# Sixteen 32x32 tiles for the random features and 128x32 tiles for the key-value state of a linear-attention block

## The chip, the cores and the metric

The kernel runs on one core of a Trainium2 chip. The metric is the device time of one execution in microseconds (us). Fewer are better.

## The reference

Input is x, two sequences of 2048 tokens of 256 features. Everything is 32-bit floating point. An adaptive layer norm, then a first half of three layers of causal linear attention, with a feed-forward part, then a second layer norm and a second half of two layers of windowed attention. Only the attention of the first half is touched by the change, and the per-feature scales of queries and keys of the second half. Cut to that:

```python
# first half, for each of 3 layers; 16 heads of 16 features, omega is 16 x 8
q, k, v = (out @ W + b, in heads, for W, b in (Wq,bq), (Wk,bk), (Wv,bv))
def favor(x, omega):                       # 16 features for each head and token
    xs = x * 16 ** -0.25
    u  = xs @ omega                        # 8 columns
    h  = 0.5 * sum(xs * xs)
    return concat([exp(u - h), exp(-u - h)]) * 16 ** -0.5
Qf, Kf = favor(q, omega), favor(k, omega)
S = running sum over tokens of Kf[m] * v[d];  z = running sum of Kf
a = (Qf . S) / (Qf . z + 1e-6)
out = layer_norm(out + a @ Wo + bo);  out = layer_norm(out + relu(out @ W1 + bf1) @ W2 + bf2)
# second half, for each of 2 layers
q = l2norm(q) * q_scale;  k = l2norm(k) * k_scale;  q, k = rotary_xpos(q, k)
```

## The kernel before

The program is written instruction by instruction, with an own order for each engine and semaphores between them. The tokens of the first half go in 24 blocks (n = 0 to 23: 8 blocks of 512 tokens for each of three layers), those of the second half in 64 units of 128 tokens. Nothing is planned at run time: the order on an engine is the order of the calls in its part of `build` (TensorE from line 613, ScalarE, VectorE, GpSimd and the DMA queue of SyncE after it), and for blocks 6 to 21 it is one loop body.

Of one block, TensorE does this, and works besides on the feed-forward part of the block before the last (`up` and `down`, laid between the attention's calls as filling):

- `proj(n, i)`, i = 0 to 3: six matmuls each into PSUM bank i. Banks 0 and 1 hold the keys' two halves of 128 features (m = 0, 1), banks 2 and 3 the queries'. A product in float32r is made of three matmuls on a high and a low part (`mm3`).
- ScalarE's `operands(n, i)` (lines 1901 to 1904) adds the bias and makes for each bank two tiles `OPS[i]`, A and B: of the 128 features 64 are kept as they are beside their 64 squares. Partitions change places in it, so it takes four activations of 64 partitions. It signals `a_sq`.
- `values(n, i)`: the values into banks 0 and 1; VectorE's `add_bv` (line 3185) writes them to `VP` and signals `d_v`.
- `favor(n, i, bank)`: u - h and -u - h for 128 of the features. Two matmuls of true fp32 with 128 rows and 64 columns on 512 tokens each. Their weights are `OM`: 128 x 128 numbers of omega, its negative, and -1/8 where a square enters. GpSimd's `features_of` makes `OM` once a layer. Order on the banks: 2, 3 for the keys, 0, 1 for the queries. It signals `e_fv`.
- ScalarE's `features(n, i, bank)` (lines 1913 to 1919): one exponential for each bank of keys (`FK`), three for each of queries (`FQ`). It signals `a_fe`.
- `attn_out` of the block before, `turn_k` (transposes of `FK`, line 477, copied to `KS` by ScalarE, line 1948), then for j = 0 to 3 `scores(n, j)` (32 rows x 128 columns, four row groups), which VectorE masks into `U` (line 3175), and `sums(n, j)`.
- `sums(n, j)` works in bank 4: two matmuls with the state `SBD`, then two that add the tile's keys times values to the state (weights `KS`, 128 x 128, moving `VP`, 128 columns; into columns 256 to 511; only the 16x16 blocks on the diagonal are wanted), then sixteen matmuls of 128 rows x 32 columns with `VP` and `U`. VectorE's `state` (line 3167) multiplies columns 256 to 511 with a block mask into `TMP`, and GpSimd (line 4627) adds that to `SBD`. For every sixteenth tile there is no update.

A float32 matmul stands in the trace as two records of MATMUL and two of LDWEIGHTS, a float32r one and a transpose as one of each.

```python
            mm(e, PS[0:64, bank, :], OM[:, l % 2, 0:64], OPS[i][0], True)
            mm(e, PS[64:128, bank, :], OM[:, l % 2, 64:128], OPS[i][1], True).then_inc(*e_fv.up(n, i))
```

Between the halves SyncE's queue (lines 5387 to 5400) loads the second half's first weights (`load_piece`, line 5286), tables of the rotation (`load_table`, line 5372) and the scales (`load_scales`, line 5385, 12 DMAs into `QSB`). GpSimd's `table(u)` (line 4814) multiplies a table with `QSB`; it waits for all 12. It stands in GpSimd's order before roundings of the last feed-forward part (`RL`, line 4615).

Of the kernel before, what the change touches and what calls it, by code (L numbers as in the profile page):

```python
# [41 lines left out]
def build(nc, ctx, ins, out):  # L42
# [47 lines left out]
    QSB = sb("QSB", [128, 2, 256])  # L90
# [21 lines left out]
    GG = sb("GG", [128, 6, 512])  # L112
# [11 lines left out]
    RSLOT = (0, 1, 2, 0, 2, 1)  # L124

# [38 lines left out]
    p_om = ev("p_om", by(range(3), R2))  # L164
# [54 lines left out]
    s_bb = ev("s_bb", by(range(3), range(11)), 16)  # L219
# [147 lines left out]
    def hidden(q, hb):  # L367
        return (KT, PR, PT)[hb // 2][:, hb % 2, :] if q == NQ - 1 else GG[:, hb, :]
# [6 lines left out]
    def residual_of(q):  # L375
        return T2 if q == NQ - 1 else GG[:, 4:6, :]
# [37 lines left out]
    def _(e):  # L414
# [13 lines left out]
        def proj(n, i):  # L428
            m, nm = i % 2, "wk" if i < 2 else "wq"
            if n > 0:  # L430
                e.wait_ge(*d_am.at(n - 1, 1))
            need_weights(e, piece_of(n // 8, nm))
            for k in range(2):
                e.wait_ge(*a_x.at(n, k))
                e.wait_ge(*d_x.at(n, k))
                t = mm3(e, PS[:, i, :], [a[:, 256 * k + 128 * m:256 * k + 128 * m + 128] for a in wt(nm, 0, 512)], xt(0, k, 0, 512), k == 0)
# [69 lines left out]
        def sums(n, j):  # L506
# [105 lines left out]
        values(0, 0)  # L612
        modulate(4)
        modulate(5)
        values(0, 1)
        favor(0, 0, 2)
        favor(0, 1, 3)
        favor(0, 2, 0)
        favor(0, 3, 1)
# [19 lines left out]
        favor(1, 0, 2)  # L639
        favor(1, 1, 3)  # L640
        favor(1, 2, 0)
        favor(1, 3, 1)
# [27 lines left out]
        favor(2, 0, 2)  # L670
        favor(2, 1, 3)
        favor(2, 2, 0)
        favor(2, 3, 1)
# [34 lines left out]
        values(3, 0)  # L708
        up(1, 2)
        values(3, 1)  # L710
        favor(3, 0, 2)
        favor(3, 1, 3)
        favor(3, 2, 0)
        favor(3, 3, 1)
# [40 lines left out]
        favor(4, 0, 2)  # L755
        favor(4, 1, 3)
        favor(4, 2, 0)
        favor(4, 3, 1)
# [38 lines left out]
        favor(5, 0, 2)  # L797
        favor(5, 1, 3)
        favor(5, 2, 0)
        favor(5, 3, 1)  # L800
# [27 lines left out]
        for n in range(6, 22):  # L828
# [7 lines left out]
            down(m, 0)  # L836
            up(m, 2)
            down(m, 1)
            values(n, 1)
            favor(n, 0, 2)  # L840
            favor(n, 1, 3)
            favor(n, 2, 0)
            favor(n, 3, 1)
# [273 lines left out]
        favor(22, 0, 2)  # L1117
        favor(22, 1, 3)
        favor(22, 2, 0)
        favor(22, 3, 1)  # L1120
# [38 lines left out]
        favor(23, 0, 2)  # L1159
        favor(23, 1, 3)  # L1160
        favor(23, 2, 0)
        favor(23, 3, 1)
# [723 lines left out]
    def _(e):  # L1886
# [4 lines left out]
        def operands(n, i):  # L1891
            l, m = n // 8, i % 2
            lo, hi = slice(0, 64), slice(64, 128)
            col = BC[:, l % 2, (2 if i < 2 else 0) + m:(2 if i < 2 else 0) + m + 1]
            if i == 0:
                e.wait_ge(*s_bb.at(l, 10))
# [3655 lines left out]
```

## Time and profile before

| | us |
|---|---|
| median of 3 executions | 2650.11 |
| lowest, highest | 2649.51, 2653.05 |
| the profiled execution, its own time | 2656.85 |
| its span in the profile | 2655.1 |
| TensorE busy in it | 2580.7 (97%) |

The profile is of one execution. Its page and its views give busy times of each engine, in all or in a stretch; groups of instructions with their mean duration; the chain of work that ended last; and the instructions in order of time, in which neighbours of a kind are merged (a row "x12" begins with its first and its length goes to the end of the last). A matmul's record is longer than the distance to the next, since matmuls are pipelined: starts are compared, not ends.

### The profile page before, as it was taken

Reading aid. Unit: us, or ns where it says so; the run is one execution under the profiler, and the core shown is the slowest. Engines: PE = TensorE matmul, PEld = TensorE weight load, DVE = VectorE, ACT = ScalarE, POOL = GpSimd, SP = SyncE. Lnnn points to the kernel's source line nnn. Section 1 sums busy time; section 2 is a strip of 40 time slices with the busy share of each in tenths; the row PEclk is TensorE's granted clock in tenths of the full one; section 3 lists DMA queues with packets and bytes.
Section 4 is the critical chain, followed back from the end, with each engine's and each line's share of the span. In section 5 each row is a group of like instructions: output and inputs, shape, how many; then the busy total and the mean of one; then the engine's idle time right before and its main releaser. Section 6 shows DMA issues by size and latency. Waiting matters only on the chain.

```text
span 2655.1 us, 61404 instructions
## 1 busy us (share of the span) xinstructions
PE 2580.7 (97%) x21288; PEld 2131.3 (80%) x21288; DVE 2119.8 (80%) x5244; ACT 1545.6 (58%) x3137; POOL 1426.2 (54%) x1406
## 2 busy tenths in 40 slices
PE   7899999999999999999898999999999999999998
PEld 4688888888888888888786788888888887888886
DVE  5688877787677777888899888888898887888775
ACT  3454445444554455444446777777767777777772
POOL 2253443444343345444476766666666666776664
PEclk9899999999999999999999999999999999999999
DMA  3100000010000010000111000000110110110001
GB/s 93 33 17 10 17 2 17 9 35 6 1 1 8 12 31 25 18 17 26 47 50 52 29 12 19 16 14 19 31 35 23 34 35 22 35 32 26 27 29 48
DMA packets 78976, 67.17 MB, mean 25 GB/s; under 512 B 15800, under 2 KB 73272, under 8 KB 78680
## 3 DMA queue, kind: packets, MB, share of 16 engines
q1 hardware_dynamic: 78680, 63.25, 8.1%
q8 instruction: 182, 2.98, 0.5%
q14 instruction: 114, 0.93, 0.1%
HBM read 49.18 MB, written 12.58 MB: 23 GB/s over the span
## 4 chain that ended last, share of the span: by engine, by line
PE 91%; DVE 3%; issue 2%; ACT 1%; POOL 1%; SPq 0%; DMA 0%; DVEq 0%; ACTq 0%; POOLq 0%
PE PS L274 81%; PE PS L982 4%; PE PS L944 1%; PE PS L935 1%; PE PS L1012 1%; PE PS L487 1%; PE PS L425 1%; PE PS L477 1%; PE PS L893 1%; DVE PS L3583 1%; PE PS L1042 0%; ACT PR L2244 0%; DVE U L3175 0%; DVE SM L3556 0%; DVE SQ L3563 0%
## 5 line engine op out<-in xcount | busy, mean ns | idle before, releaser
L2244 ACT ACTIVATE PR<-PS,SM 128x256 f32<-128x256 f32 (+1 forms) x512 | 280.3, 559 | 137.2 <-DVE SM L3588 136.8
L1930 ACT ACTIVATE FB<-PS,BC 128x512 f32<-128x512 f32 x192 | 133.4, 695 | 326.5 <-PE PS L274 188.0
L3175 DVE TENSOR_TENSOR U<-PS,CST 128x512 f32<-128x512 f32 x384 | 238.2, 683 | 42.1 <-PE PS L274 41.7
L4615 POOL TENSOR_TENSOR RL<-FB,RH 128x512 fp32r<-128x512 f32 x96 | 126.1, 1313 | 236.0 <-DVE RH L3153 236.0
L274 PE MATMUL PS<-W2H,RH 128*128 128x256 f32 x768 | 226.0, 294 | 6.9 <-POOL RL L4615 6.9
L4837 POOL TENSOR_TENSOR SM<-SM,COL 128x8 f32<-128x8 f32 x128 | 225.6, 1763 | 10.7
L3583 DVE CUSTOM_DVE_ANT_0 PS<-PS,MSK 128x256 f32<-128x256 f32 (+1 forms) x512 | 202.6, 436 | 30.0 <-PE PS L274 28.9
L274 PE MATMUL PS<-W2H,RL 128*128 128x256 f32 x768 | 215.8, 281 | 0.0
L274 PE MATMUL PS<-W2L,RH 128*128 128x256 f32 x768 | 215.6, 281 | 0.0
L4627 POOL TENSOR_TENSOR SBD<-SBD,TMP 128x256 f32<-128x256 f32 x84 | 64.5, 768 | 217.2 <-DVE TMP L3167 217.2
L274 PEld LDWEIGHTS PS<-W2H,RH 128*128 128x128 f32 x768 | 145.1, 189 | 29.6 <-issue 25.0
L274 PE MATMUL PS<-VAH,XBH 128*128 128x512 f32 x384 | 163.3, 425 | 1.0 <-ACT SQ L2193 0.6
L274 PE MATMUL PS<-X1H,W1H 128*128 128x512 f32 x384 | 160.6, 418 | 3.1 <-ACT FB L1930 2.4
L1938 ACT COPY NUM<-PS 128x256 f32<-128x256 f32 x96 | 36.1, 376 | 200.9 <-DVE TMP L3167 173.4
L274 PE MATMUL PS<-X1L,W1H 128*128 128x512 f32 x384 | 151.7, 395 | 0.0
L274 PE MATMUL PS<-VAL,XBH 128*128 128x512 f32 x384 | 151.4, 394 | 0.0
L274 PE MATMUL PS<-VAH,XBL 128*128 128x512 f32 x384 | 151.4, 394 | 0.0
L274 PE MATMUL PS<-X1H,W1L 128*128 128x512 f32 x384 | 151.2, 394 | 0.0
L274 PE MATMUL PS<-KT,QT 64*128 64x256 f32 (+1 forms) x1024 | 142.4, 396 | 8.9 <-ACT PT L2257 6.2
L4619 POOL TENSOR_TENSOR X0L<-NUM,X0H 128x512 fp32r<-128x512 f32 x48 | 65.5, 1384 | 156.4 <-ACT X0H L1944 156.4
L274 PEld LDWEIGHTS PS<-W2L,RH 128*128 128x128 f32 x768 | 145.3, 189 | 2.4
L982 PE MATMUL PS<-CST,PR 128*128 128x128 f32 x992 | 137.6, 274 | 7.7 <-ACT PR L2244 7.6
(265 smaller groups left out, 8711.2 us busy)
## 6 DMA issues: line engine op xcount, KB each, us to landing
PX<-in_L_attn_x SPq DMA_DIRECT2D x16, 512.0 KB, 4.0
TB<-in_k_rot SPq DMA_DIRECT2D x64, 128.0 KB, 2.3
SG<-in_L_attn_W SPq DMA_DIRECT2D x24, 256.0 KB, 2.7
xp_scratch<-PX SPq DMA_DIRECT2D x8, 512.0 KB, 2.9
xs_scratch<-X SPq DMA_DIRECT2D x64, 64.0 KB, 1.5
ZS<-xs_scratch SPq DMA_DIRECT2D x16, 256.0 KB, 2.8
GG<-xp_scratch SPq DMA_DIRECT2D x7, 512.0 KB, 3.7
out<-GG SPq DMA_DIRECT2D x7, 512.0 KB, 2.9
```

Of the source, the lines that this page charges most:

```text
L274: return e.matmul(o, l, r, start=start, stop=True, skip_group_check=True)
L425: t = e.transpose(PS[:, 2 + k, 128 * j:128 * j + 128], X[:, 4 * c + j, 128 * k:128 * k + 128], IDN)
L982: m = e.transpose(PS[:, 3 + par, a:a + 128], PR[:, par, a:a + 128], IDN)
L1930: e.activation(FB[:, hb % 2, :], PS[:, 5, :], ACT.Relu, bias=BC[:, l % 2, 4 + hb:5 + hb]).then_inc(*a_re.up(n, hb))
L1938: e.copy(NUM[:, :, 128 * j:128 * j + 128], PS[:, 4, 0:256].rearrange("p (m q) -> p m q", m=2)).then_inc(*a_nu.up(n, j))
L2244: t = e.activation(PR[:, par, 256 * i + lo:256 * i + hi], PS[:, 3 + par, 256 * i + lo:256 * i + hi], ACT.Exp, bias=S[:, 40 + 2 * g + i:41 ...
L3175: e.tensor_tensor(heads(U[:, u % 6, :], 4), heads(PS[:, g, :], 4), bcast(CM, 4), ALU.mult).then_inc(*d_mk.up(n, u))
L3583: t = e.tensor_tensor_reduce(o, o, MSK[:, z:z + hi - lo], 1.0, NEG, ALU.add, ALU.max, S[:, 32 + 2 * g + i:33 + 2 * g + i])
L4615: e.tensor_tensor(RL[:, r, :], FB[:, 0, :], RH[:, r, :].bitcast(F), ALU.subtract).then_inc(*p_rl.up(n, hb))
L4619: e.tensor_tensor(X0L[:, k, :], NUM[:, k, :], X0H[:, k, :].bitcast(F), ALU.subtract).then_inc(*p_al.up(n, k))
L4627: e.tensor_tensor(SBD[:, (tile + 1) % 2, :, :], SBD[:, tile % 2, :, :], TMP[:, :, :], ALU.add).then_inc(*p_sd.up(n, j))
L4837: e.tensor_tensor(o, a, MHALF.broadcast_to([128, 8]), ALU.pow).then_inc(*h_rs[i].up(u))
```

## The change

- The columns of Wq and Wk are stored in another order (`split_parts`), so that `proj(n, i)` makes 32 features of each half of the queries and of the keys. It is the same number of matmuls; the rounding of these two weights takes two instructions for one.
- `operands` takes two activations of 128 partitions for four of 64. The biases' columns are loaded in that order (13 small DMAs for a layer where there were 11).
- `favor(n)` is one call: for each of the four row groups (r = 2, 3, 0, 1) and each bank's operands (c = 0 to 3) one 32x32 matmul with omega's block on the plain features, and then sixteen more with the -1/8 block on the squares, into the same banks. It begins when all operands and both halves of the values are there. `OM` shrinks to a block that repeats, so `features_of` takes one instruction for two.
- In `sums` the update of the state is eight matmuls of 128 rows x 32 columns on 32 columns, into 64 columns of bank 4 for 256. `state` reads these 64 columns four times each.
- `values(n, 1)` goes before the calls that stood between it and `values(n, 0)` (in block 0 the last two products of the modulation, in blocks 3 and 6 to 21 one or two feed-forward calls).
- `QSB` moves behind `GG` (which gives its first plane to `G0`, at the place of `QSB`). Layer 0's scales are loaded before block 16, layer 1's at unit 4 of the second half, after `load_norm(0)`. `table(u)` waits for the six DMAs of layer 0 only while u < 32.

```diff
     def split_parts(p):
+        if phase == 1 and at < 1024:
+            def places(w, k):
+                return w[:, 512 * k:512 * k + 512].rearrange("p (s t m f) -> p t m s f", s=4, t=2, m=2)[:, at // 512, :, :, :]
+            return [(places(WQH, k), places(WQL, k), s[:, 256 * k:256 * k + 256].rearrange("p (m s f) -> p m s f", m=2, s=4)) for k in range(2)]
...
-        def favor(n, i, bank):
+        def favor(n):
             l = n // 8
-            e.wait_ge(*p_om.at(l, 1))
-            e.wait_ge(*a_sq.at(n, i))
-            if i < 2:
-                e.wait_ge(*a_sq.at(n, 2 + i))
-            else:
-                e.wait_ge(*d_v.at(n, i - 2))
-            mm(e, PS[0:64, bank, :], OM[:, l % 2, 0:64], OPS[i][0], True)
-            mm(e, PS[64:128, bank, :], OM[:, l % 2, 64:128], OPS[i][1], True).then_inc(*e_fv.up(n, i))
+            e.wait_ge(*p_om.at(l))
+            for i in range(4):
+                e.wait_ge(*a_sq.at(n, i))
+            for i in range(2):
+                e.wait_ge(*d_v.at(n, i))
+            for r in BANKS:
+                for c in range(4):
+                    mm(e, PS[32 * c:32 * c + 32, r, :], OM[32 * r:32 * r + 32, l % 2, 0:32], OPS[c][0][32 * r:32 * r + 32, :], True)
+            for i, r in enumerate(BANKS):
+                for c in range(4):
+                    t = mm(e, PS[32 * c:32 * c + 32, r, :], HO[32 * r:32 * r + 32, 0:32], OPS[c][1][32 * r:32 * r + 32, :], False)
+                t.then_inc(*e_fv.up(n, i))
...
                 for m in range(2):
-                    mm(e, PS[:, 4, 256 + 128 * m:384 + 128 * m], KS[:, j // 2, D * (j % 2) + 128 * m:D * (j % 2) + 128 * m + 128],
-                           value_places(VP[:, j, :])[:, 4 * m:4 * m + 4, :, :], not started and m == 0)
+                    for g in range(4):
+                        a = D * (j % 2) + 128 * m + 32 * g
+                        mm(e, PS[32 * g:32 * g + 32, 4, 256 + 32 * m:288 + 32 * m], KS[:, j // 2, a:a + 32],
+                               value_places(VP[:, j, :])[:, 4 * m + g, :, :], not started and m == 0)
...
             A, B = OPS[i]
-            e.activation(A[lo, :], PS[lo, i, :], ACT.Identity, bias=col[lo, :])
-            e.activation(B[hi, :], PS[hi, i, :], ACT.Identity, bias=col[hi, :])
-            e.activation(A[hi, :], PS[lo, i, :], ACT.Square, bias=col[lo, :])
-            e.activation(B[lo, :], PS[hi, i, :], ACT.Square, bias=col[hi, :]).then_inc(*a_sq.up(n, i))
+            e.activation(A, PS[:, i, :], ACT.Identity, bias=col)
+            e.activation(B, PS[:, i, :], ACT.Square, bias=col).then_inc(*a_sq.up(n, i))
...
-                e.wait_ge(*t_qs.at(11))
-                e.tensor_tensor(TB[:, u % 2, :], TB[:, u % 2, :], QSB[:, u // 32, :], ALU.mult).then_inc(*h_tb.up(u))
+                e.wait_ge(*t_qs.at(11 if u >= 32 else 5))
+                e.tensor_tensor(TB[:, u % 2, :], TB[:, u % 2, :], QSB[:, 1 - u // 32, :], ALU.mult).then_inc(*h_tb.up(u))
...
+        load_scales(0)
         for n in range(16, 21):
...
         load_piece(P2 + 1)
         load_table(0)
-        load_scales(0)
-        load_scales(1)
         load_piece(P2 + 2)
...
                 load_norm(0)
+                load_scales(1)
```

## Rows read from the trace of the kernel before

**Rows 1.** The page: the span, and busy times of the engines

```profile
span 2655.1 us, 61404 instructions
...
PE 2580.7 (97%) x21288; PEld 2131.3 (80%) x21288; DVE 2119.8 (80%) x5244; ACT 1545.6 (58%) x3137; POOL 1426.2 (54%) x1406
```

**Rows 2.** Busy times of PE, PEld, DVE, ACT, POOL in most of the first half

```profile
110.00:1250.00 1140.00, 1137.92 (x10753) 944.96 (x10749) 891.90 (x1905) 561.26 (x929) 485.06 (x454) 1.00 0.05 15
```

**Rows 3.** The chain that ended last, 110 to 1250 us, by line

```profile
by line: PE PS L274 94.5%; PE PS L487 1.9%; PE PS L425 1.7%; PE PS L477 1.6%; ACT FB L1930 0.1%; DVE U L3175 0.1%; issue 0.1%
```

**Rows 4.** TensorE in order of time, block 11: start, length, tiles, rows*columns

```profile
621.11 2.80 PE L274 MATMUL PS<-U,OM 128*64 128x512 f32 x12
623.73 1.03 PE L274 MATMUL PS<-KS,OM 128*64 128x512 f32 x4
624.69 0.50 PE L274 MATMUL PS<-X1H,W1H 128*128 128x512 f32 x1
...
629.87 0.48 PE L274 MATMUL PS<-X1H,W1H 128*128 128x512 f32 x1
...
631.42 1.15 PE L274 MATMUL PS<-FQ,FK 32*128 32x256 f32 x16
```

**Rows 5.** Line 274 (source view), the first 0.2 us of scores(11, 0)

```profile
L274 PE MATMUL PS<-FQ,FK x4: 478/478/478, 631.4 to 631.4; 32*128 32x256 f32 x4
```

**Rows 6.** TensorE in order of time in sums(11, 1)

```profile
642.40 0.61 PE L274 MATMUL PS<-VP,KS 128*128 128x128 f32 x4
642.95 1.08 PE L274 MATMUL PS<-U,VP 128*32 128x128 f32 x32
```

**Rows 7.** ScalarE in order of time, block 11

```profile
610.14 0.69 ACT L1901 ACTIVATE U<-PS,BC 64x512 f32<-64x512 f32 x1 [0.77 <-PE PS L274]
...
620.62 0.68 ACT L1904 ACTIVATE KS<-PS,BC 64x512 f32<-64x512 f32 x1
...
623.08 1.26 ACT L1919 ACTIVATE FK<-PS,COL 128x512 f32<-128x512 f32 x2
...
627.07 0.74 ACT L1915 ACTIVATE FQ<-PS,COL 128x512 f32<-128x512 f32 x1
627.64 0.74 ACT L1930 ACTIVATE FB<-PS,BC 128x512 f32<-128x512 f32 x1
```

**Rows 8.** VectorE in order of time between two masks

```profile
639.48 2.48 DVE L3175 TENSOR_TENSOR U<-PS,CST 128x512 f32<-128x512 f32 x4
...
644.09 0.42 DVE L3167 TENSOR_TENSOR TMP<-PS,CST 128x256 f32<-128x256 f32 x1 [1.08 <-PE PS L274]
...
645.17 2.48 DVE L3175 TENSOR_TENSOR U<-PS,CST 128x512 f32<-128x512 f32 x4 [0.32 <-PE PS L274]
```

**Rows 9.** TensorE in order of time, block 1

```profile
76.30 1.08 PE L274 MATMUL PS<-U,OM 128*64 128x512 f32 x4 [0.72 <-ACT U L1904]
...
87.57 0.60 PE L477 MATMUL PS<-CST,FK 128*128 128x128 f32 x4
89.04 1.15 PE L274 MATMUL PS<-FQ,FK 32*128 32x256 f32 x16 [0.88 <-ACT KS L1948]
```

**Rows 10.** SyncE's queue in order of time between the halves

```profile
1307.90 0.48 SPq L5372 DMA_DIRECT2D TB<-in_k_rot  x1
1308.42 1.50 SPq L5385 DMA_DIRECT2D QSB<-in_L_ffn_q_scale  x3
...
1312.81 1.38 SPq L5385 DMA_DIRECT2D QSB<-in_L_ffn_k_scale  x3
```

**Rows 11.** GpSimd in order of time between the halves

```profile
1318.96 0.88 POOL L4814 TENSOR_TENSOR TB<-TB,QSB 128x256 f32<-128x256 f32 x1 [15.70 <-DMA QSB<-in_L_ffn_k_scale]
1319.80 1.44 POOL L4615 TENSOR_TENSOR RL<-FB,RH 128x512 fp32r<-128x512 f32 x1
```

**Rows 12.** TensorE between the halves, the end of its longest gap

```profile
1321.49 0.55 PE L274 MATMUL PS<-W2H,RH 128*128 128x256 f32 x1 [6.85 <-POOL RL L4615]
```

**Rows 13.** DMAs of 1303 to 1325 us: size, median us to landing

```profile
TB<-in_k_rot SPq DMA_DIRECT2D x1, 128.0 KB, 5.4
```

More of the change, by code:

```diff
@@ L89, in build @@
     TB = sb("TB", [128, 2, 256])
-    QSB = sb("QSB", [128, 2, 256])
+    G0 = sb("G0", [128, 512])
     MSK = sb("MSK", [128, 384])
@@ L111, in build @@
     HTH, HTL = sb("HTH", [128, 2, 512], FR), sb("HTL", [128, 2, 512], FR)
-    GG = sb("GG", [128, 6, 512])
+    GG = sb("GG", [128, 5, 512])
+    QSB = sb("QSB", [128, 2, 256])
     PS = ctx.enter_context(nc.psum_tensor("PS", [128, 8, 512], F))
@@ L162, in build @@
     d_rh, d_rl = ev("d_rh", by(S24, R8)), ev("d_rl", by(S24, (1, 3, 5, 7)))
-    p_om = ev("p_om", by(range(3), R2))
+    p_om = ev("p_om", by(range(3)))
     p_xb, p_hb, p_al, p_zq = (ev(f"p_{k}", by(S24, R2)) for k in ("xb", "hb", "al", "zq"))
@@ L218, in build @@
     s_row = [ev(f"s_row{i}", by(range(3)), 16) for i in range(7)]
-    s_bb = ev("s_bb", by(range(3), range(11)), 16)
+    s_bb = ev("s_bb", by(range(3), range(13)), 16)
     s_x = ev("s_x", [("p", c) for c in S8] + [("r", n) for n in CH3], 16)
@@ L375, in residual_of @@
     def residual_of(q):
[L376 removed]
+        return T2 if q == NQ - 1 else GG[:, 3:5, :]
     def gate_bank(q, hb):
@@ L612, in _ @@
         values(0, 0)
+        values(0, 1)
         modulate(4)
         modulate(5)
[L615 to L619, printed above, removed]
+        favor(0)
         turn_k(0, 0)
@@ L638, in _ @@
         values(1, 1)
[L639 to L642, printed above, removed]
+        favor(1)
         attn_out(0, 0)
@@ L669, in _ @@
         up(0, 2)
[L670 to L673, printed above, removed]
+        favor(2)
         up(0, 3)
@@ L708, in _ @@
         values(3, 0)
+        values(3, 1)
         up(1, 2)
[L710 to L714, printed above, removed]
+        favor(3)
         up(1, 3)
@@ L754, in _ @@
         up(2, 3)
[L755 to L758, printed above, removed]
+        favor(4)
         attn_out(3, 0)
@@ L796, in _ @@
         up(3, 3)
[L797 to L800, printed above, removed]
+        favor(5)
         attn_out(4, 0)
@@ L836, in _ @@
             down(m, 0)
+            values(n, 1)
             up(m, 2)
             down(m, 1)
[L839 to L843, printed above, removed]
+            favor(n)
             up(m, 3)
@@ L1116, in _ @@
         down(20, 1)
[L1117 to L1120, printed above, removed]
+        favor(22)
         up(20, 3)
@@ L1158, in _ @@
         down(21, 1)
[L1159 to L1162, printed above, removed]
+        favor(23)
         up(21, 3)
@@ L5360, in store_scaled, with load_scales @@
             e.dma_start(xp_d[4 * c:4 * c + 4].rearrange("t p d -> p t d"), PX.rearrange("p i (t d) -> p (i t) d", t=2)).then_inc(*s_xp.up(n))
+        def load_scales(l):
+            for i, nm in enumerate(("q", "k")):
+                v = ins[f"L0_ffn_{nm}_scale"][l:l + 1, :]
+                for z, (a, b, n) in enumerate(((0, 0, 64), (64, 32, 32), (96, 0, 32))):
+                    e.dma_start(QSB[:, 1 - l, 128 * i + a:128 * i + a + n], v[:, b:b + n].broadcast_to([128, n])).then_inc(*t_qs.up(6 * l + 3 * i + z))
+        load_scales(0)
         for n in range(16, 21):
@@ L5379, in load_norm @@
                 e.dma_start(B2[:, i, :], ins["L0_ffn_" + nm][l:l + 1, :].broadcast_to([128, D])).then_inc(*t_b2.up(l, i))
-        def load_scales(l):
-            for i, nm in enumerate(("q", "k")):
-                v = ins[f"L0_ffn_{nm}_scale"][l:l + 1, :]
-                for z, (a, b, n) in enumerate(((0, 0, 64), (64, 32, 32), (96, 0, 32))):
-                    e.dma_start(QSB[:, l, 128 * i + a:128 * i + a + n], v[:, b:b + n].broadcast_to([128, n])).then_inc(*t_qs.up(6 * l + 3 * i + z))
         load_again(21)
@@ L5507, in constants @@
     sign = np.where(i % 16 < 8, 0.5, -0.5).astype(f)
-    other = (((i[:, None] + 64) % 128) // 16 == i[None, :] // 16).astype(f) * f(-0.125)
-    cst = np.stack([np.eye(128, dtype=f), blk, other, (i[:, None] <= i[None, :]).astype(f), blk * sign[None, :]], axis=1)
+    pairs = (i[:, None] % 32 // 16 == i[None, :] % 32 // 16).astype(f)
+    cst = np.stack([np.eye(128, dtype=f), blk, pairs * f(-0.125), (i[:, None] <= i[None, :]).astype(f), pairs * sign[None, :]], axis=1)
     c = np.arange(32)
```

40 lines of the change are left out of this document (21 added, 19 removed).

## The prediction

> **What bounds the kernel now.** I read the page first: TensorE is busy for 97% of the span, no other engine for more than 80% [rows 1]. Its busy time is that of pipelined records, so the chain of waits was read next. From 110 to 1250 us it is TensorE's alone: its lines make up 99.7% of the chain [rows 3], and it is busy for 1137.9 of 1140 us, with VectorE at 78%, ScalarE at 49% and GpSimd at 43% [rows 2]. So in blocks 2 to 23 time taken out of TensorE's stream is time won, until another engine's chain becomes the later one. The other stretches have limits of their own: block 1 waits for ScalarE [rows 9], and between the halves TensorE stands for 6.85 us for a rounding by GpSimd [rows 12], which stood behind a DMA of the scales [rows 11]. The second half proper is not touched.
>
> **The features on TensorE.** Before, eight fp32 matmuls leave 16 records, from 621.11 us to 624.69, where the next call starts: 3.58 us [rows 4]. A slot is the distance between starts on one tile. The first twelve records take 2.80 us and the next four start at 623.73, so twelve records in six slots took 2.62 us: 0.43 us a slot, two column tiles at once. Eight slots are 3.44 us; the rest is a first weight load and the change of tile shape at the end. After, 32 matmuls leave 64 records. If all sixteen tiles run beside one another, that is two matmuls a tile, two records each: 4 slots, 1.72 us. That tiles do run beside one another is seen for four: in `scores` 16 records of 32 rows take 1.15 us together [rows 4], and four begin within the same 0.1 us, each 0.48 us long [rows 5]. No row has both row and column tiles. Bounds: 1.72 us (all sixteen at once), and above no concurrency beyond a few tiles (rivals below). I take 4 slots, since with four row tiles and with four column tiles [rows 4, 6] nothing but the slots is seen. I add 0.1 us for starting sixteen tiles in turn and 0.1 us for weight load and change of shape (an estimate: the 3.58 us above held 0.14 for that): 1.94 us, 1.64 us less for each block.
>
> A rule of the Trainium skill speaks against this. The page "TensorE: Matmul & The Clock Gate", Part 3 on packing small matmuls, says that matmuls start and end strictly in program order. By that rule the two passes of a matmul, on one tile, would hold up all that is behind them; what it would cost is a rival. By it the 16 records of `scores` could not overlap by four, and rows 4 and 5 show that they do.
>
> **What the block loses again.** ScalarE's exponentials follow each other by 0.57 us (from the first `FK` at 623.08 to the last `FQ` at 627.07 are seven steps [rows 7]). Before they began 1.97 us after `favor`. After, all four banks come at once, about 2.1 us after it. So they are hardly earlier, while TensorE is 1.64 us earlier. The relu behind them ended at 628.38 [rows 7] and TensorE wanted it at 629.87 [rows 4]: slack 1.49 us. It becomes 1.49 - 1.64 - 0.15 = -0.3 us. I count 0.3 us of new wait a block. Net 1.34 us. The operands themselves go from 16 to 8 activations of 0.70 us a block, done before from 610.14 to 621.30 [rows 7], just in time for `favor`. The freed 5.6 us are off the path (ScalarE is at 49%) and pay only in block 1. They also mean that waiting for all operands at once costs nothing: they are then bounded by `proj`, which ends over 5 us before. The values' second half moves ahead of feed-forward calls, so `d_v` is not late either; what moves behind it is filling whose inputs were there.
>
> **The state's update.** Before, 4 records from 642.40 to the next start at 642.95: 0.55 us, of it 0.44 for four slots of 0.11 and 0.1 for the change of shape, which stays but moves in front [rows 6]. After, 16 records on four column tiles, 4 slots. A slot of 128 columns is about 0.11 us; here are 32 columns. Bounds: a quarter of that, 0.03 us a slot, or no less than now, 0.11 us (no gain); nothing is added, since the number of slots stays. I take 0.04 us, nearer the quarter, as in `favor` and `sums` the slot goes with the columns (0.43 us for 512, 0.11 for 128): 0.28 us less for each tile. VectorE has 0.32 and 1.08 us idle in a round of `sums` [rows 8] and its masks ended at 641.96, 0.99 us before they were wanted at 642.95 [rows 6, 8]; four tiles take 1.1 us from a block but each has a round of its own to catch up. So I keep it whole. `state` reads 64 columns four times for 256 once: 0.42 us as before [rows 8].
>
> **The two first blocks.** Block 0: ScalarE sets the pace; keys' exponentials start about 1 us later, the last ends about 0.2 us later. Block 1: TensorE was ready at 75.6 us (76.30 less 0.72 of waiting) and reached `scores` at 89.04 [rows 9]. After, operands are ready; the last exponential ends 2.15 + 7 x 0.57 + 0.74 = 6.9 us after the start, and the last transposes, their copy and the start of `scores` take 89.04 - 87.57 = 1.47 us as before [rows 9]: 84.0 us, 5 us won.
>
> **Between the halves.** The 12 DMAs of the scales hold SyncE's queue from 1308.42 to 1314.19 [rows 10], and GpSimd waited until 1318.96 for the last of them [rows 11]. After, GpSimd waits only for the table, issued at 1307.90 [rows 10]; it lands 5.4 us later, 1313.3 [rows 13]. So its product and the rounding behind it come 5.7 us earlier. The gap is 6.85 us [rows 12]. Bounds 0 to 5.7 us: VectorE is nearly full just there and may not follow. I take 4.5 us. The six DMAs put at unit 4 take 2.9 us of the queue (half of 5.8), at a place where the queue waits for the end of the first half; nothing there is wanted soon. The six put before block 16 stand before reloads of x, wanted long after.
>
> **At the start** two more DMAs (0.48 us each by the same rows) and four more rounding instructions: 0 to 1.5 us, I take 0.5.
>
> **Sum.** Features, blocks 2 to 23: 22 x 1.34 = 29.5. State, 82 of their 88 tiles: 82 x 0.28 = 23.0. Block 1: 5.0, block 0: -0.2. Handover 4.5, start -0.5. Together 61.3 us. The profiled execution of 2656.85 us would take 2595.5; the median of the runs lies 6.74 us below it, so 2650.1 - 61.3 = 2588.8 us. That is 2.3%; a measurement here tells some 0.2% (5 us) from no change.
>
> **Rivals.**
> - *Another chain takes over* (10%). ScalarE's or VectorE's chain behind `favor` costs 1.3 us a block, not 0.3: 22 us more, 2611. For it: the slack of 1.49 us is used up. Against: all engines but TensorE are under 80%.
> - *Features not faster* (9%). Only eight tiles at once: 8 slots, as before, with no new waits. 61.3 - 29.5 - 1.6 = 30 us won, 2620.
> - *Row groups one after the other* (3%), the case on the other side. Four column tiles run together but the next row group waits for both passes: 8 groups x 2 slots x 0.43 = 6.9 us, 3.3 us more a block. 2620 + 24 x 3.3 = 2699. It decides from 1.25 us a block on (30 / 24), a `favor` of 4.8 us. For it: no row mixes the two tilings.
> - *Strict order* (2%). A tile's second record waits for its first, and only the next tile's first runs beside it: 33 slots, 14.2 us, 10.6 us more a block, 2874 us. Against: rows 4 and 5. It is the rule named above.
> - *The change does not shorten what it seems to*: the state's slots stay at 0.11 us. That is 23 us, and lies in the range.
>
> **Numbers.** The forecast has 76%: 2588.8, and alone a range of 2577 to 2605 (state at 0.03 us a slot, no new waits, the whole gain at the handover: 11 us lower; no gain at the handover and half of the state's: 16 us higher). To leave out 2 in 10 at most I reach to the first rival: 2574 to 2612. Faster by over 0.2%: 0.94 (forecast, first two rivals); slower by over 0.2%: 0.05; within: 0.01.
>
> **What would show it.** 64 records of 32*32 a block, from first to next call 1.9 us; rows of `KS` as 128*32 in about 0.2 us; 96 activations of 128x512 in place of 64x512 for each of two lines; the relu behind the exponentials within 0.3 us of its use; no wait of GpSimd for `QSB`. A `favor` over 3 us, TensorE busy under 98% in the first half, or a gap of over 3 us left between the halves would show steps wrong.

## The result, and the profile of the changed kernel

The changed kernel takes 2636.76 us (median of 4 runs, 2633.62 to 2638.52), the kernel before 2650.36 beside it: a ratio of 0.9946, 95% interval 0.993 to 0.9962. It is faster by 13.6 us where 61.3 had been forecast, and 48 us above the forecast of 2588.8. The profiled execution took 2638.52 us, its span 2636.7. The page after, with the line that answers to [rows 1]:

```profile
span 2636.7 us, 65564 instructions
...
PE 2530.9 (96%) x23520; PEld 2096.4 (80%) x23520; DVE 2130.5 (81%) x5253; ACT 1403.9 (53%) x2945; POOL 1425.5 (54%) x1406
```

TensorE's busy time fell by 49.8 us and the span by only 18.4: the rest came back as idle time. The stretch of [rows 2] shows where:

```profile
110.00:1250.00 1140.00, 1111.26 (x12796) 928.92 (x12796) 911.47 (x1933) 442.72 (x768) 495.45 (x459) 0.99 0.05 15
```

Of 1140 us TensorE is idle for 28.7, where it was idle for 2.1 before, and the granted clock is 0.99 of full, not 1.00. What TensorE waited for from 150 to 1250 us, all of it before and the three largest waits after (engine, line, releaser: us in total, times, longest us):

```profile
PE PS L274 <- ACT FB L1930: 0.2, 1, 0.2
```

```profile
PE PS L276 <- DVE VP L3169: 22.8, 17, 3.3
PE PS L276 <- issue: 1.7, 2, 0.8
PE PS L276 <- DVE X1L L3011: 1.6, 2, 1.2
```

One new wait makes up nearly all of it: 17 times TensorE stands for line 3169, `add_bv`, VectorE's bias add that takes the values out of PSUM. It stands in front of the features, which now write into those banks all at once. In this text a *gap* is the distance between the start of the features and the start of the last matmul before them; it is 0.21 us where TensorE doesn't wait. Before, every block from 6 to 23 had 0.21. After, the ordinary blocks have 0.79, and blocks 6, 10, 11, 18, 20, 21 and 23 have 2.15 to 3.57; only block 22 kept 0.21. TensorE in block 12 after:

```profile
665.82 0.28 PE L276 MATMUL PS<-W2H,RL 128*128 128x256 f32 x1
666.61 0.63 PE L276 MATMUL PS<-U,OM 32*32 32x512 f32 x3 [0.52 <-DVE VP L3169]
...
666.72 0.61 PE L276 MATMUL PS<-KS,OM 32*32 32x512 f32 x1
667.04 0.62 PE L276 MATMUL PS<-U,OM 32*32 32x512 f32 x3
...
667.47 0.84 PE L276 MATMUL PS<-U,CST 32*32 32x512 f32 x3
...
667.91 0.61 PE L276 MATMUL PS<-KS,CST 32*32 32x512 f32 x1
...
668.36 0.59 PE L276 MATMUL PS<-KS,CST 32*32 32x512 f32 x1
668.88 0.50 PE L276 MATMUL PS<-X1H,W1H 128*128 128x512 f32 x1
```

The features themselves do what the change says. Sixteen tiles start within 0.11 us (666.61 to 666.72), the next record on the first tile 0.43 us later, and from first to next call it is 2.27 us where it was 3.58 [rows 4].

The state's update, which answers to [rows 6] (block 12):

```profile
685.56 0.61 PE L276 MATMUL PS<-FQ,SBD 128*128 128x128 f32 x4
686.10 0.33 PE L276 MATMUL PS<-VP,KS 128*32 128x32 f32 x16
686.25 1.18 PE L276 MATMUL PS<-U,VP 128*32 128x128 f32 x32
```

From the start of the `KS` records to the next start it is 0.15 us where it was 0.55. From the start of the `SBD` records in front of them to `KS` it is 0.54 us, where it was 0.44 before. That makes about 0.29 us less a tile.

Between the halves, answering to [rows 11] and [rows 12]: GpSimd waits for the table itself, and TensorE's gap shrank from 6.85 us to 1.89.

```profile
1300.27 0.74 POOL L4796 TENSOR_TENSOR TB<-TB,QSB 128x256 f32<-128x256 f32 x1 [10.59 <-DMA TB<-in_k_rot]
1300.97 1.71 POOL L4597 TENSOR_TENSOR RL<-FB,RH 128x512 fp32r<-128x512 f32 x1
```

```profile
1302.94 0.35 PE L276 MATMUL PS<-W2H,RH 128*128 128x256 f32 x1 [1.89 <-POOL RL L4597]
```

**Why VectorE is late.** VectorE in order of time, in block 11 before and in block 12 after (for both, the second `VP` line is the values' second half):

```profile
616.41 1.66 DVE L3014 SCALAR_TENSOR_TENSOR Z<-Z,ST,BB 128x256 f32<-128x256 f32 x4
618.16 1.67 DVE L3022 SCALAR_TENSOR_TENSOR X<-Z,ST,BB 128x256 f32<-128x256 f32 x4
621.22 0.76 DVE L3185 TENSOR_TENSOR VP<-PS,BB 128x256 f32<-128x256 f32 x2 [1.38 <-PE PS L274]
```

```profile
660.66 0.76 DVE L3169 TENSOR_TENSOR VP<-PS,BB 128x256 f32<-128x256 f32 x2 [4.27 <-PE PS L276]
661.33 1.67 DVE L2997 SCALAR_TENSOR_TENSOR Z<-Z,ST,BB 128x256 f32<-128x256 f32 x4
663.09 2.71 DVE L3005 SCALAR_TENSOR_TENSOR X<-Z,ST,BB 128x256 f32<-128x256 f32 x4
665.72 0.74 DVE L3169 TENSOR_TENSOR VP<-PS,BB 128x256 f32<-128x256 f32 x2
```

Before, the second half was written from 621.22 to 621.98, that is 0.87 us *after* the features had begun at 621.11 [rows 4], and nobody minded: only the fourth pair waited for it, 2.6 us in. After, the first matmul waits for it. What VectorE itself waited for before was TensorE: its products were done at 619.83, and then it stood idle for 1.38 us until the values' matmuls had come. The change moves these matmuls forward, so the add could follow the products at once and end at about 620.6, 0.5 us ahead of the features (an estimate from these rows: 619.83 + 0.76). So in an ordinary block the eight products of `norm2_b` ahead of the add leave it in time, with little to spare. In blocks 6, 10, 18 and 21 they don't: there VectorE was not idle before the add in the kernel before either. In block 10, where weight splits come on top, the products ended 0.2 us after the features' start (566.84):

```profile
565.36 1.67 DVE L3022 SCALAR_TENSOR_TENSOR X<-Z,ST,BB 128x256 f32<-128x256 f32 x4
566.95 0.76 DVE L3185 TENSOR_TENSOR VP<-PS,BB 128x256 f32<-128x256 f32 x2
```

The second thing is that after, in block 12, the four products of `X` take 2.71 us instead of 1.67. The source view of line 3005 for those four, and of the same line before:

```profile
L3005 DVE SCALAR_TENSOR_TENSOR X<-Z,ST,BB x4: 478/482/1519, 663.1 to 664.3; 128x256 f32<-128x256 f32 x4
```

```profile
L3022 DVE SCALAR_TENSOR_TENSOR X<-Z,ST,BB x4: 479/480/484, 618.2 to 619.4; 128x256 f32<-128x256 f32 x4
```

One product of the four took 1519 ns, the others 480. GpSimd ran `X0L` at the time (a view of each kernel, GpSimd in order of time):

```profile
664.09 2.84 POOL L4601 TENSOR_TENSOR X0L<-NUM,X0H 128x512 fp32r<-128x512 f32 x2 [6.82 <-ACT X0H L1927]
```

```profile
622.02 2.75 POOL L4619 TENSOR_TENSOR X0L<-NUM,X0H 128x512 fp32r<-128x512 f32 x2 [9.39 <-ACT X0H L1944]
```

Before, ScalarE had 16 activations for the operands and came to the cast that feeds `X0L` only at 621.33, so GpSimd began 0.9 us after the features. With 8 activations ScalarE casts at 663.39, and GpSimd begins 2.5 us ahead of them, beside VectorE's products. The Trainium skill says of this, on the page "SBUF — State Buffer", section "SBUF: two separate sides", that VectorE and GpSimd share a pair of ports, and that a VectorE operation with two inputs in SBUF and a GpSimd operation that reads SBUF exclude each other for a whole instruction. The trace agrees in kind: one product, with inputs `Z` and `BB`, is longer by 1.04 us, against 1.4 us of one `X0L` that had begun 0.19 us before it (GpSimd's spans are rough). These 1.04 us are more than the 0.5 us to spare in an ordinary block; in blocks 11 and 20 two products take about 1.5 us each beside `X0L`, and the gap is 2.16 and 2.15.

**The clock.** Behind the long gaps TensorE's granted clock falls to half (1.2 GHz). Three of seven such places after block 5 (stretch, length, busy times, and PEclk as the number before the last two):

```profile
556.00:563.00 7.00, 6.07 (x69) 2.77 (x70) 2.55 (x6) 2.16 (x4) 0.00 (x0) 0.52 0.35 42
614.00:618.00 4.00, 4.00 (x53) 2.00 (x37) 1.08 (x1) 1.80 (x4) 0.00 (x0) 0.58 0.02 4
1092.00:1096.00 4.00, 4.00 (x39) 1.95 (x9) 1.94 (x2) 2.66 (x5) 0.00 (x0) 0.59 0.05 17
```

The features there take 3.13 to 4.00 us instead of 2.27. Before, the granted clock from 110 to 1250 us was 1.00 of full [rows 2].

### The profile page after: what moved, and what is told of

It is laid out like the page before. It is cut to its first block, busy times and chain, and to the rows that moved or that the text cites. A ratio compares the mean times of both kernels' runs of the same rounds, so it can differ in the third digit from the quotient of the medians.

```text
span 2636.7 us, 65564 instructions
## 1 busy us (share of the span) xinstructions
PE 2530.9 (96%) x23520; PEld 2096.4 (80%) x23520; DVE 2130.5 (81%) x5253; ACT 1403.9 (53%) x2945; POOL 1425.5 (54%) x1406
## 4 chain that ended last, share of the span: by engine, by line
PE 49%; DVE 5%; issue 3%; POOL 2%; ACT 1%; DMA 0%; SPq 0%; DVEq 0%; ACTq 0%; POOLq 0%
PE PS L276 41%; PE PS L974 4%; PE PS L936 1%; PE PS L927 1%; PE PS L1004 1%; PE PS L885 1%; DVE PX L3005 1%; DVE PS L3567 1%; PE PS L1034 1%; ACT PR L2227 0%; DVE ST L2986 0%; DVE SQ L3547 0%; DVE SM L3540 0%; POOL ST L4566 0%; DVE Z L2997 0%
## 5 line engine op out<-in xcount | busy, mean ns | idle before, releaser
L4597 POOL TENSOR_TENSOR RL<-FB,RH 128x512 fp32r<-128x512 f32 x96 | 126.2, 1315 | 221.5 <-DVE RH L3136 221.5
L276 PEld LDWEIGHTS PS<-W2H,RL 128*128 128x128 f32 x768 | 144.9, 189 | 0.0
L4832 POOL TENSOR_TENSOR OTL<-OO,OTH 128x512 fp32r<-128x512 f32 x64 | 82.9, 1295 | 105.4 <-ACT OTH L2263 105.4
```

The lines of the kernel that those rows point to most:

```text
L276: return e.matmul(o, l, r, start=start, stop=True, skip_group_check=True)
L4597: e.tensor_tensor(RL[:, r, :], FB[:, 0, :], RH[:, r, :].bitcast(F), ALU.subtract).then_inc(*p_rl.up(n, hb))
L4832: e.tensor_tensor(OTL[:, :], OO[:, :], OTH[:, :].bitcast(F), ALU.subtract).then_inc(*h_ol.up(u))
```

## The experiments

Theory A: the late bias add of the values, an order on VectorE, costs the missing gain. A2: it is late because GpSimd's earlier `X0L` slows VectorE. B: VectorE's queue is simply full, so that what is moved back is wanted as much. C: the sixteen tiles themselves bring the lower clock. D: moving the values' matmuls is to blame.

### vp_first: the values' bias add first

In VectorE's loop over blocks 6 to 21:

```
+            add_bv(n, 1)
             splits(n, "v")
             if z >= 0: norm2_b(z)
-            add_bv(n, 1)
```

> Blocks 6 to 21: VectorE writes the second half of VP before the weight splits and the second norm's two products, nothing else. Theory A (TensorE waits before favor because that write is late in VectorE's queue, and its clock falls to half after the longest of these waits): the waits before favor, 22 us over 0.21 us a block in these 16 blocks, go, and with them five or six of the seven stretches at half clock, 7 us in favor and some more behind it: 28 to 35 us less, about 2605. Theory B (VectorE's queue is simply full, so what moves back is wanted as much): under 8 us less. Theory C (the clock falls because of the 32x32 tiles, whatever the wait): the waits go, 22 us less, but the stretches at half clock stay.

Measured: 2605.89 us (4 runs), ratio 0.983 (0.9814 to 0.9846). TensorE's waits for `VP` from 150 to 1250 us:

```profile
PE PS L276 <- DVE VP L3169: 4.7, 2, 3.0
```

The two left are blocks 3 and 23, outside the loop. In blocks 6 to 22 every gap is 0.21, the features take 2.28 us, and the clock never falls. 31 us came back by moving one line of VectorE's order; the gaps of blocks 6 to 21 sum to 3.3 us instead of 25.6, and their features take 7.2 us less. A is confirmed. B, with under 8 us, and C fall: the same tiles run at full clock. VectorE in block 12:

```profile
651.89 0.76 DVE L3169 TENSOR_TENSOR VP<-PS,BB 128x256 f32<-128x256 f32 x2 [0.34 <-PE PS L276]
652.56 3.72 DVE L3005 SCALAR_TENSOR_TENSOR X<-Z,ST,BB 128x256 f32<-128x256 f32 x4
```

The products are even slower here (3.72 us), and nobody waits for them: the slow products hurt only through what stood behind them.

### x0l_late: GpSimd waits for the products

```
+            e.wait_ge(*d_nb.at("2", z))
             low_attention(w, 0)
```

> Blocks 6 to 21: GpSimd's low part of the attention (X0L) waits until VectorE has done the second norm; nothing else. Theory A2 (GpSimd's X0L beside it stretches VectorE's four products X from 1.67 to 2.7 or 3.7 us, and that is what makes VP late): these products take 1.7 us again, the wait before favor goes from 0.58 to about 0 in the ordinary blocks and falls by 1 to 2 us in the others, 10 to 20 us less. Rival (the products are long for another reason, or VP is late because of what stands in front alone): under 5 us, products as long as before.

Measured: 2611.51, ratio 0.9853 (0.9838 to 0.9867).

```profile
650.22 1.67 DVE L3005 SCALAR_TENSOR_TENSOR X<-Z,ST,BB 128x256 f32<-128x256 f32 x4
651.81 0.74 DVE L3169 TENSOR_TENSOR VP<-PS,BB 128x256 f32<-128x256 f32 x2
```

With GpSimd held back the products take 1.67 us again. The add comes in time in ordinary blocks and in blocks 11 and 20 (gap 0.21); in block 12 it ends at 652.55, 0.6 us ahead of the features at 653.16. Blocks 6, 10, 18 and 21 have 0.86, 1.45, 1.32 and 1.43, without a fall of the clock: there the add is late without `X0L` too (in block 6 two products are slow beside another GpSimd operation, as before the change). So in most blocks both are needed for the loss, an order that leaves about half a microsecond, and a neighbour that takes 1 us. Either edit alone mends most. The gain of 25 us is larger than the 10 to 20 expected: 18.0 of it are gaps of blocks 6 to 21, and 7.3 their features, which the clock had made longer.

### vp_first_x0l_late: both

> Both edits. Theory A with A2: little more than the better of the two, under 5 us, since either takes the wait before favor away in ordinary blocks. If VectorE's time is what binds (theory B), the two add up, since only this one gives VectorE time back.

Measured: 2607.32, ratio 0.9836 (0.9821 to 0.985), no clear difference from the first: nothing is left for the second edit to win.

### values_late: the values' matmuls where they were before

In TensorE's loop `values(n, 1)` stands behind `down(m, 1)` again, right ahead of the features.

> Blocks 6 to 21: the values' second half is again made right before favor, as in the kernel before. X0L then starts later, so VectorE's products are short again, but favor now waits for both halves of VP, which come about 1.1 us after the values. Theory A: a wait of 0.9 to 1.3 us in each block and none of 2 to 3.5, so no stretch at half clock in these blocks: between 8 us less and 3 us more than the change. Theory that the earlier values cost nothing: 15 us more.

Measured: 2621.05, ratio 0.9892 (0.9877 to 0.9907): 15.7 us better than the change, and my expectation of about no difference was wrong. All blocks 6 to 21 now have a gap of 1.22 to 1.45 us, more than the 0.79 of ordinary blocks in the change, but no long ones, and no half clock behind them. VectorE's `X` products take 1.67 us there in block 12 and the others like it. So the sum of the gaps of these blocks is 20.1 us instead of 25.6, and the features of the same blocks take 7.4 us less: 12.9 of the 15.7 us. D holds in part: with VectorE's order as it was, the move cost 15.7 us. It isn't to blame by itself, since vp_first keeps it and is 15.2 us faster than this run: the matmuls have to be forward *with* their add.

### before_reordered: the same order in the kernel before

> The kernel before with the same move in VectorE's order as helped the change: the bias add of the values' second half ahead of the weight splits and norm products in blocks 6 to 21. If that order is only a debt that the change made due (the features used to wait for the second half of the values at their fourth pair alone), nothing is won here: the gap before the features is 0.21 us already, 2649 to 2651.5. If the order is better by itself, 2640 or less, and the change's own features part is then overrated by that.

Measured: 2653.11 (10 runs) against 2650.05, ratio 1.0012 (1.0003 to 1.0021). The order is worth nothing, or slightly less than nothing, by itself (2649 to 2651.5 was expected). It was a debt that the change made due.

### state_alone, handover_alone, vp_first_no_state: the terms priced

`state_alone` is the kernel before with the change's two hunks for the state's update (TensorE's eight matmuls and VectorE's mask on compact blocks).

> The kernel before, with only the state's update of the change: eight matmuls of 32 output columns on 128x32 tiles in place of two of 128, and the mask read from the compact blocks. The prediction's term is 82 updates x 0.28 us = 23.0 us, all of it on TensorE's own path, so 2627.5 us. In the change's trace the group of KS matmuls went from 0.54 to 0.15 us and the one after it from 0.44 to 0.54, 0.29 net: by that 2626.8. If the shorter update makes another engine late (VectorE's masks or the scans), less than 18 us comes out and the gap stands before the state's or the score's matmuls. No lower clock is expected, since nothing before the features changes.

Measured: 2623.83, ratio 0.9901 (0.9885 to 0.9917): 26.3 us. Block 11's matmuls:

```profile
630.35 0.33 PE L274 MATMUL PS<-VP,KS 128*32 128x32 f32 x16
630.49 1.06 PE L274 MATMUL PS<-U,VP 128*32 128x128 f32 x32
```

From the features of block 2 to those of block 23 it takes 1113.0 us where the kernel before takes 1137.2, 24.2 less. In that stretch 79 tiles have an update (84 less the last tile of blocks 3, 7, 11, 15 and 19), so it is 0.31 us for each, a little more than the 0.29 of the rows. Another 11 updates stand in blocks 0, 1 and 23.

`handover_alone` is the kernel before with the scales' new place and times.

> The kernel before, with only the scales moved: QSB at its new place, six loads before the sixteenth block and six after the first norm load, G0 apart from GG. The prediction's term is 4.5 us, from TensorE's gap of 6.85 us before the second half's first rotated operands. In the change's trace that gap was 1.89 us. Expected 2645.7 to 2646.2. A rival: the six loads on SyncE ahead of block sixteen's delay a load there, then the gain is under 3 us and a block about 16 is longer.

Measured: 2645.55 (12 runs), ratio 0.9981 (0.9973 to 0.999): 4.6 us, where the term was 4.5. The interval is wide beside it, about 2.6 to 7.2 us.

`vp_first_no_state` is the reordered kernel with the state's update of before.

> The change with VectorE's bias add of the values' second half ahead of the norm products and weight splits in blocks 6 to 21, and with the state's update as before the change: so it holds the features' part and the handover's. With the state's term at 23 to 24 us it should take 2605.9 + 23.5 = 2629.4 us. Below the kernel before by 21: 4.5 of handover, the rest features, where the prediction had 29.5 + 5.0 of block 1; what is missing are the gaps before the features in blocks 1, 3 and 23 (5.6, 2.1 and 3.3 us) and the features' 2.27 us in place of 1.94. If the two parts help each other or stand in each other's way it differs from 2629.4 by more than 3.

Measured: 2629.06, ratio 0.9923 (0.9905 to 0.9941), and 2629.4 was expected: the parts add up. Less the handover the features' part is worth 16.5 us, with the gaps of blocks 1, 3 and 23 still in it.

### vp_all: blocks 1, 3 and 23 as well

```
-        norm2_b(0)
-        splits(3, "v")
         add_bv(3, 0)
         add_bv(3, 1)
+        norm2_b(0)
+        splits(3, "v")
```
the same in block 23, and in block 1 `add_bv(1, 1)` ahead of `modulate_b(2)`.

> As the reordered kernel of blocks 6 to 21 (2605.9 us), and the same in blocks 1, 3 and 23: the bias add of the values stands ahead of the next block's modulation in block 1, and ahead of the norm products and weight splits in blocks 3 and 23. Gaps before the features there were 5.61, 2.07 and 3.30 us; if each falls to about 0.3 and block 23's features run at full clock (2.28 against 3.76), 5 + 1.8 + 3.0 + 1.5 = 11 us come back: 2595. If another wait stands right behind the add (the casts of ScalarE, the scans), only a part does: 2600 to 2604. If the delayed norm products hold up turning of x in the next block, a block period after 3 or 23 grows.

Measured: 2598.17 (2596.95 to 2598.75), ratio 0.9802 (0.9788 to 0.9815), the fastest kernel of the study: 52.0 us below the one before, 38.6 below the change. Its page:

```profile
span 2595.2 us, 65564 instructions
...
PE 2516.7 (97%) x23520; PEld 2089.7 (81%) x23520; DVE 2134.4 (82%) x5253; ACT 1403.5 (54%) x2945; POOL 1428.2 (55%) x1406
```

No wait for `VP` is listed from 150 to 1250 us. Gaps: 2.52 in block 1, 0.48 in block 3, 0.21 in 23, whose features take 2.28. It is 3 short of the hope. In block 1 TensorE now waits 2.2 us for ScalarE's operands. So it does in the change's own profile, where that gap is 2.52 too; in vp_first and five other profiles with the same block 1 it waits for the values and the gap is 5.6. No run tells what decides between the two, so no gain is shown for the edit in block 1.

### split_wait and split_vp_all: the features in two halves

Row groups 2 and 3 (both passes) wait for the operands alone; the waits for `d_v` stand in front of row groups 0 and 1.

```
-            for i in range(2):
-                e.wait_ge(*d_v.at(n, i))
-            for r in BANKS:
+            for h in range(2):
+                if h:
+                    for i in range(2):
+                        e.wait_ge(*d_v.at(n, i))
+                for r in BANKS[2 * h:2 * h + 2]:
...
```

> The change with VectorE's order untouched, but the features in two halves: row groups 2 and 3 (both passes, 16 matmuls) wait for the operands alone, and the waits for the two halves of the values stand in front of row groups 0 and 1. One half takes 4 slots of 0.43 = 1.7 us. In ordinary blocks (values late by 0.58 us) the second half enters while the first runs, on other rows: features of about 2.3 us with no gap, so 0.6 us a block back; in blocks 6, 10, 11, 18, 20, 21 and 23, late by 2 to 3.4 us, 1.7 us of it is hidden, and the late half adds its own 1.7, so about 0.6 back too, but TensorE is no longer idle for over 1.9 us and the clock should hold, which gives 1 to 1.7 us more in each. Sum: 16 x 0.6 + 7 x 1.9 = 23: 2614. If a wait for all operands at once is not what cost the time, it stays at 2637. If the halves don't overlap, ordinary blocks lose about 1.1 us and it is over 2645.

Measured: 2630.44, ratio 0.9918 (0.9903 to 0.9934): 6.3 us below the change, not 23.

> The fastest so far (2598.2 us, the values' bias add first in blocks 1, 3, 6 to 21 and 23) with the features in halves as well. Nothing is late there but in blocks 1 (2.5 us) and 2 (0.9 us), so if the two halves share the array freely, it is 2597 to 2600. If sixteen tiles need to be started in the order of their passes to run side by side (first pass of all row groups, then second), the features take up to 3.4 us in place of 2.28 and the time is 2598 + 22 x 1.1 = 2622.

Measured: 2606.12, ratio 0.983 (0.9814 to 0.9847): 8 us slower than with all tiles at once, between the two times forecast. Both runs say the same. With nothing late the features take 3.03 us in halves and 2.28 at once. TensorE in the second of these kernels:

```profile
649.51 0.62 PE L276 MATMUL PS<-U,OM 32*32 32x512 f32 x3
...
650.15 0.58 PE L276 MATMUL PS<-U,OM 32*32 32x512 f32 x1
650.39 0.60 PE L276 MATMUL PS<-U,CST 32*32 32x512 f32 x3
...
651.97 0.62 PE L276 MATMUL PS<-U,CST 32*32 32x512 f32 x3
652.02 0.59 PE L276 MATMUL PS<-KS,CST 32*32 32x512 f32 x1
652.54 0.50 PE L276 MATMUL PS<-X1H,W1H 128*128 128x512 f32 x1
```

The halves overlap by a part only (two whole halves would be 3.4 us), so the 0.58 us of wait that is hidden in an ordinary block costs 0.75 of features. Why they don't overlap more is not shown. In split_wait the long waits stand inside the features, which take 3.6 to 6.8 us there, and the clock still fell in blocks 6, 10, 21 and 23. Here a wait for everything at once is cheaper than a split one, as long as what it waits for is in time.

### graded_delay and graded_gaps: what brings the lower clock

> The reordered kernel of blocks 6 to 21 with 5, 6, 7, 8, 9, 10 and 12 extra adds of 128x256 (0.41 us each, written to the unused table buffer) in VectorE ahead of the bias add of the values' second half, in blocks 8, 10, 12, 14, 16, 18 and 20. There are 1.8 us of slack, so gaps before the features of about 0.7, 1.2, 1.6, 2.0, 2.5, 2.9 and 3.8 us. Theory: the lower clock in the change's features comes of the length of TensorE's idle time right before them; then it stays at full speed in the first blocks and falls in the last ones, the border between 2.07 (no fall in block 3) and 2.15 us (a fall in block 20). Rival: it comes of what else runs at those places (norm products, weight splits), then it doesn't fall in any of these blocks, which all had it high. The features should take 2.28 us at full clock and 3.2 to 4.0 after a fall.

The kernel that ran under this label held none of the extra adds: it is vp_first once more, and its single run took 2604.01 us, beside 2605.89. It says nothing on the question, which graded_gaps puts:

```
+            if i:
+                for k in range(RP.get(n, 0)):
...
+                    e.tensor_tensor(TB[:, 0, :], PS[:, i, 0:256], row(0), ALU.add)
```

> The reordered kernel of blocks 6 to 21 (2605.9 us) with 5, 6, 7, 8, 9, 10 and 12 extra adds of 128x256 (0.41 us each, written to the unused table buffer, each waiting for the one before) in VectorE ahead of the bias add of the values' second half, in blocks 8, 10, 12, 14, 16, 18 and 20. There are 1.8 us of slack, so gaps before the features of about 0.6, 1.0, 1.4, 1.8, 2.2, 2.7 and 3.5 us, 13 us in sum (0.06 more for each add if the waits on VectorE itself cost that). Theory: the lower clock comes of the length of TensorE's idle time right before the features; it then stays high in the first blocks and falls in the last ones, the border near 2.1 us (2.07 us gave no fall in block 3, 2.15 a fall in block 20 of the change), and the features take 2.28 us before the border, 3.2 to 4.0 behind it: 2606 + 12 + 3 x 1.3 = 2622. Rival: it comes of what else ran at those places in the change, then the features take 2.28 us in all seven blocks and it is 2618 or less.

Measured: 2620.53, ratio 0.9883 (0.9866 to 0.9899). Gaps and features (first to next call), in us:

| block | 8 | 10 | 12 | 14 | 16 | 18 | 20 |
|---|---|---|---|---|---|---|---|
| gap | 0.59 | 1.10 | 1.51 | 1.96 | 2.42 | 2.93 | 3.79 |
| features | 2.27 | 2.27 | 2.27 | 2.27 | 2.27 | 3.12 | 4.00 |

The start of the features in blocks 16, 18 and 20, and the stretches around them:

```profile
868.49 0.63 PE L278 MATMUL PS<-U,OM 32*32 32x512 f32 x3 [2.15 <-DVE VP L3176]
...
974.57 0.62 PE L278 MATMUL PS<-U,OM 32*32 32x512 f32 x3 [2.65 <-DVE VP L3176]
...
1083.10 1.07 PE L278 MATMUL PS<-U,OM 32*32 32x512 f32 x3 [3.52 <-DVE VP L3176]
```

```profile
868.40:871.40 3.00, 2.91 (x67) 1.41 (x68) 1.87 (x6) 0.74 (x2) 0.00 (x0) 1.00 0.02 5
974.50:978.50 4.00, 3.93 (x66) 1.60 (x67) 3.59 (x9) 1.11 (x2) 0.00 (x0) 0.68 0.02 6
1083.00:1088.00 5.00, 4.90 (x66) 1.88 (x67) 2.14 (x6) 0.99 (x2) 0.00 (x0) 0.50 0.31 108
```

The theory holds in its first part: a longer gap brings the fall, in blocks that were at full clock without it (18 and 20; the rival had 2.27 us in all seven). Its border near 2.1 us doesn't: three falls had been expected, and block 16 had none. A fall costs 1.4 us in block 18 (its period, from features to features, is 53.2 us instead of 51.8) and 1.9 in block 20 (53.7 instead of 51.8). No single length is the border: 2.42 us in block 16 left the clock alone, as did 2.52 in block 1 of the change, and in the change gaps of 2.16 and 2.15 in blocks 11 and 20 brought it down. What else decides there is open.

## Why the prediction was wrong

**The step that failed** is in "What the block loses again": "The values' second half moves ahead of feed-forward calls, so `d_v` is not late either". It put the new wait for the values at nothing, and it cost 27.2 us in gaps. (That "waiting for all operands at once costs nothing" holds for ScalarE's operands, which were in time in these blocks.) The step looked at TensorE's order only. `d_v` is raised by VectorE, whose order the diff leaves alone, and there eight products of 0.4 us, in some blocks weight splits too, stand ahead of the add. The trace of before had both halves of the answer. In blocks 6, 10, 18 and 21 the add was late by what stands ahead of it, `X0L` or not (0.65 to 1.24 us more than 0.21 are left of the gap in x0l_late). In ordinary blocks there was half a microsecond to spare, and a second step took it: "The freed 5.6 us are off the path" left out that ScalarE's freed time lets GpSimd's `X0L` begin 2.5 us ahead of the features, beside VectorE's products, which then take 1.04 us more. From the features of block 2 to those of block 23 the time fell from 1137.2 us to 1128.0:

| part, in that stretch | us |
|---|---|
| features shorter and `scores` later behind them, 21 x (1.30 - 0.19) | -23.3 |
| state's update (state_alone) | -24.2 |
| gaps before the features, over the kernel before, blocks 3 to 23 | +27.2 |
| features above 2.28 us, blocks 2 to 22 (1.8 of it in blocks 4 and 5, the rest at the lower clock) | +9.0 |
| the rest (mostly between features and `scores`: about 1.6 in the blocks at the lower clock, 1.1 waiting for `FQ` in blocks 5 and 22, -0.4 in 3 and 4) | +2.1 |
| sum | -9.2 |

In blocks 4 and 5 the clock was full; TensorE stood 0.84 us after the last features there, and the profile shows nothing that it waited for. So it is the gaps first and the clock second. The rival "another chain takes over" (10%) had the mechanism, VectorE's chain, but behind `favor` and at 1.3 us a block; it stood ahead of `favor`, at 0.58 us in ordinary blocks and up to 3.4 in seven others, and the clock came on top. That VectorE slows beside GpSimd was in no step.

**The other terms:**
- *Features on TensorE.* Sixteen tiles at once, 4 slots, as taken. 1.30 us won a block, not 1.64: predicted 1.94, measured 2.27. The term mis-sized is the 0.1 us for starting the tiles in turn. In the third slot the starts spread from 667.47 to 667.91, so the last tile is 0.4 us late, and the shape's change comes behind it. The strict order (2%) and the row groups in turn (3%) are refuted: the first would have cost 10.6 us a block by the prediction's estimate, and the features became 1.3 us shorter. The Trainium skill ("TensorE: Matmul & The Clock Gate", Part 3) states that matmuls start and end in program order. The traces don't agree for these fp32 matmuls: in split_vp_all a record of the second half (the seventeenth with `OM`; the first half has sixteen) starts at 650.15, before the first half's matmuls with `CST` at 650.39. The same part's table has sixteen tiles packed side by side, which the trace shows.
- *New wait behind them.* Predicted 0.3 us a block; from features to `scores` it is 0.19 longer (6.92 against 6.73). It stands where it was expected: in block 12 the relu behind the exponentials ends at 674.10, and TensorE's next call starts at 674.24, 0.24 us after the last transpose where it was 0.03.
- *State.* Predicted 0.28 us a tile, measured 0.29 in the rows and 0.31 on average; 23.0 predicted in all, 26.3 by itself. The sum did not count the 8 updates of blocks 0 and 1. That the slot goes with the columns came out: four slots in 0.15 us.
- *First blocks.* Predicted 4.8; the features of block 2 start at 128.4 us instead of 133.8, 5.4 less. This agreement is luck as far as one can tell: state_alone, whose features are those of before, has them at 126.2, and each profile has stretches of lower clock of other lengths there.
- *Handover.* Predicted 4.5, measured 4.6 alone, 4.96 in the gap.
- *Start.* Predicted 0.5 us lost; the features of block 0 start at 30.80 us instead of 30.81, so nothing was.

With the order mended the sum comes to 52.0 of 61.3. What is left is mainly 0.34 us x 22 = 7.5 in the features, partly set off by the state, and gaps in blocks 1 and 2 (2.52 and 0.91 us). The marks that the prediction named did show it: TensorE at 97.5% of the first half, under the 98% named, while the features stayed under 3 us in ordinary blocks and the gap between the halves fell below 3.

## What to carry to other kernels

When one instruction's wait is replaced by one for all its inputs, or a use is moved earlier, take every producer's *end* against the new use, in the producer's own queue and with its inputs where they will then be: here that left half a microsecond in an ordinary block and less than nothing in four others, and with what followed the order of that queue cost 31 us. A move on one engine's order needs its counterpart on the others', and here one line did it. And engine time that is freed starts other work earlier: ask whom it will then run beside.

## What the hardware showed unexpectedly

- A VectorE product of 480 ns took 1519 ns beside GpSimd's `X0L` (four in 2.71 to 3.72 us instead of 1.67); with GpSimd held back it is 1.67 us again.
- Sixteen 32x32 tiles share TensorE for fp32 matmuls: 64 records of 32x512 in 2.27 us. Given in two halves of eight tiles they take 3.03 us, and records of the second half start among those of the first.
- TensorE's clock fell to half behind single gaps of 2.93 and 3.79 us and not behind 0.59 to 2.42 in the same kernel, but behind 2.15 in another; a fall cost 1.4 to 1.9 us of a block, beyond the gap.
